# Five of eight repeats of a transformer block's attention stage, rolled from unrolled code into a hardware loop on four engines

## The reference, cut to what matters

```python
x = x + attention(layernorm(x), wq, wk, wv, wo)     # x: 8 sequences x 256 positions x 256
x = x + moe(layernorm(x), gate_w, w1, w3, w2, sw1, sw3, sw2)

# attention: 16 heads of 128, rotary embedding on q and k, causal softmax
q, k, v = (einsum('bsd,dnh->bsnh', x, w) for w in (wq, wk, wv))
q, k = llama_rope(q) / sqrt(128), llama_rope(k)
probs = softmax(where(causal, einsum('bqnh,bknh->bnqk', q, k), -1e30))
out = einsum('bqnh,nhd->bqd', einsum('bnqk,bknh->bqnh', probs, v), wo)

# moe: 8 experts of width 176, the best two of each token, and a shared expert of width 352
scores = softmax(x @ gate_w.T); topk_w, topk_idx = top_k(scores, 2)
y = sum over the two of w2_e(silu(w1_e x) * (w3_e x)) * topk_w / sum(topk_w)
y = y + (silu(x @ sw1) * (x @ sw3)) @ sw2
```

## Time and profile before

| what | value |
| --- | --- |
| median of three runs | 812.82 us |
| lowest and highest | 811.15 and 814.33 us |
| the profiled execution's own time | 814.33 us |
| its span, from first to last instruction | 812.5 us |
| mean granted TensorE clock | 0.980 |
| instructions in the trace | 16293 |

### The profile page before, as it was taken

One profiled execution on the slowest core, in us unless ns is written; L12 is line 12 of the kernel. 1 busy time (PEld: TensorE's weight loads), 2 busy tenths in 40 slices (PEclk: granted clock), 3 DMA queues, 4 the chain that ended last, 5 costly groups with the idle time before them and its releaser, 6 DMA issues.

```text
span 812.5 us, 16293 instructions
## 1 busy us (share of the span) xinstructions
PE 752.0 (93%) x5520; PEld 701.4 (86%) x5520; DVE 639.6 (79%) x1765; ACT 532.9 (66%) x1663; POOL 482.6 (59%) x508
## 2 busy tenths in 40 slices
PE   3799999999999999999999999999996879999994
PEld 3788999998998999899999989998885868888884
DVE  5698989988897998899888979988995574444447
ACT  4688777767776776777677767677886434555531
POOL 3578666676667666666766676667776261433300
PEclk9899999999999999999999999999999988999997
DMA  7254344444000000000000000001322213333373
GB/s 225 54 170 130 136 184 170 168 163 176 15 1 27 1 14 15 14 14 2 21 8 14 1 28 2 14 14 32 86 73 82 64 40 97 106 106 113 103 246 104
DMA packets 35753, 61.59 MB, mean 76 GB/s; under 512 B 6744, under 2 KB 27192, under 8 KB 35096
## 3 DMA queue, kind: packets, MB, share of 16 engines
q1 hardware_dynamic: 31624, 49.14, 18.6%
q0 software_dynamic: 4048, 11.42, 3.9%
HBM read 47.03 MB, written 32.46 MB: 98 GB/s over the span
## 4 chain that ended last, share of the span: by engine, by line
PE 57%; DVE 19%; POOL 11%; issue 5%; ACT 4%; DMA 3%; SPq 1%; POOLq 0%; DVEq 0%
PE bank L528 44%; DVE work L875 5%; POOL work L425 5%; PE bank L568 3%; POOL qkt_lo L1403 3%; PE bank L561 3%; DVE work L868 2%; PE bank L577 2%; DVE work L884 2%; PE bank L728 2%; POOL rows_by_expert L1516 2%; DVE pt_lo L896 2%; DMA stage<-in_L_attn_wk 1%; ACT qkt_hi L1223 1%; DVE w_lo L842 1%
## 5 line engine op out<-in xcount | busy, mean ns | idle before, releaser
L1403 POOL TENSOR_TENSOR qkt_lo<-work,qkt_hi 128x512 fp32r<-128x512 f32 x128 | 165.7, 1295 | 99.3 <-ACT qkt_hi L1223 99.3
L425 POOL TENSOR_TENSOR work<-work 128x512 f32<-128x512 f32 x127 | 165.3, 1302 | 72.0 <-DVE work L875 64.3
L875 DVE TENSOR_TENSOR work<-bank,sinn 64x512 f32<-64x512 f32 x256 | 176.2, 688 | 3.4
L528 PE MATMUL bank<-xnt_hi,w_lo 128*128 128x256 f32 x512 | 146.9, 287 | 3.2 <-POOL w_lo L1463 3.0
L1223 ACT CAST qkt_hi<-work 128x512 fp32r<-128x512 f32 x128 | 79.5, 621 | 103.1 <-POOL work L425 102.4
L528 PE MATMUL bank<-xnt_hi,w_hi 128*128 128x256 f32 x512 | 146.5, 286 | 0.0
L528 PE MATMUL bank<-xnt_lo,w_hi 128*128 128x256 f32 x512 | 146.5, 286 | 0.0
L1230 ACT ACTIVATE work<-work,bias 128x128 f32<-128x128 f32 (+1 forms) x256 | 112.6, 441 | 0.0
L868 DVE TENSOR_TENSOR work<-bank,cosn 128x512 f32<-128x512 f32 x128 | 87.8, 686 | 22.1 <-PE bank L528 22.0
L528 PEld LDWEIGHTS bank<-xnt_hi,w_lo 128*128 128x128 f32 x512 | 99.6, 195 | 3.9 <-DVE xnt_lo L906 3.3
L528 PEld LDWEIGHTS bank<-xnt_hi,w_hi 128*128 128x128 f32 x512 | 99.9, 195 | 0.0
(11 more groups left out here) (151 smaller groups left out, 2175.5 us busy)
## 6 DMA issues: line engine op xcount, KB each, us to landing
rows_by_expert<-in_zero_t SPq DMA_DIRECT2D x8, 2056.0 KB
stage<-rows_by_expert SPq DMA_DIRECT2D x39, 128.5 KB
stage<-in_L_ffn_w SPq DMA_DIRECT2D x32, 88.0 KB, 2.0
rows_by_expert<-in_zero_t SPq DMA_DIRECT2D x2, 1028.0 KB
resid<-in_L_attn_x SPq DMA_DIRECT2D x8, 256.0 KB, 3.8
stage<-in_L_attn_wq SPq DMA_DIRECT2D x8, 256.0 KB, 3.4
stage<-in_L_attn_wk SPq DMA_DIRECT2D x8, 256.0 KB, 4.2
stage<-in_L_attn_wv SPq DMA_DIRECT2D x8, 256.0 KB, 3.8
```

What stands on the lines that cost most here:

```text
L425: eng.tensor_tensor(roped[:, a], rope_cos[:, a], rope_sin[:, a], ALU.add).then_inc(rope_add, 1)
L528: mm = pe.matmul(out, lhs[a], rhs[b], start=start and n == 0, stop=stop and n == 2, skip_group_check=more)
L875: op = nc.vector.tensor_tensor(rope_sin[lo:lo + 64, a], p_qk[a][hi:hi + 64, :, :], sn, ALU.mult)
L1403: nc.gpsimd.tensor_tensor(qkt[a][1][:, :, :], roped[:, a], qkt[a][0][:, :, :], ALU.subtract).then_inc(qkt_lo, 1)
```

## The change

On PE, DVE, ACT and POOL the Python loop over b = 1 to 7 becomes: one unrolled call for b = 1, a hardware loop (`Fori`) for b = 2 to 6 whose body is in the stream once, and one unrolled call for b = 7. In the body, b is a value in a register of each engine. On DVE four waits get a `nop(nofuse=True)` behind them: one in each step of `sequence`, and one in each of the helpers `norm_mv`, `rows_stats` and `rows_mv`. They are in all eight sequences, in the loop and outside it.

```diff
@@ PE @@
             sequence(FIRST)
             pe.wait_ge(route_in, 64)
             pe.wait_ge(order_set, 1)
-            for b in range(1, B):
+
+            sequence(1)
+            with pe.Fori(2, LAST) as b:
                 sequence(b)
+            sequence(LAST)
@@ DVE @@
             def norm_mv(b):
                 dve.wait_ge(stats_done, b + 1)
+                dve.nop(nofuse=True)
                 for t in range(ST):
                     op = nc.vector.bn_aggr(mv[:, t, :], stats[:, t, :])
@@
                     if b is not LAST or h + 2 < N:
                         dve.wait_ge(s_ps, j0 + h + 3)
+                        dve.nop(nofuse=True)
                         mask_and_max((h + 2) % N)
@@
             def rows_stats(n, b):
                 dve.wait_ge(resid_done, n)
+                dve.nop(nofuse=True)
@@
             def rows_mv(n):
                 dve.wait_ge(stats2_done, n)
+                dve.nop(nofuse=True)
@@
             sequence(FIRST)
             dve.wait_ge(route_in, 64)
-            for b in range(1, B):
+
+            sequence(1)
+            with dve.Fori(2, LAST) as b:
                 sequence(b)
+            sequence(LAST)
@@ ACT @@
             sequence(FIRST)
-            for b in range(1, B):
+
+            sequence(1)
+            with act.Fori(2, LAST) as b:
                 sequence(b)
+            sequence(LAST)
@@ POOL @@
             pool.wait_ge(own_in, 16)
-            for b in range(1, B):
+
+            sequence(1)
+            with pool.Fori(2, LAST) as b:
                 sequence(b)
+            sequence(LAST)
             pool.wait_ge(scattered, 64 * (B - 1))
```

## The result

The changed kernel took 817.30 us (median of 4 runs, 816.66 to 818.66), the kernel before 812.52 beside it (4 runs, 811.15 to 814.33). The ratio is 1.0059, with an interval of 1.0035 to 1.0084: 4.8 us slower, between 2.8 and 6.8. The forecast was slower, 823.9: the direction is right, and the cost is less than half of the 11.1 us forecast.

The account below looks back on a forecast made before the run. The prediction took PE to bound the five looped sequences, with 1.1 us idle in each. Jumps 9.2 + 0.2, registers 1.7 and nops 0 made 11.1 us more, 823.9 us; own range 818 to 831, 8 in 10 815 to 837.

Parts of the forecast that it names:

- What it adds, 1: the jump back: At four loop borders each engine rereads its block; POOL's 2.3 us per jump reaches PE: 9.2 us, plus 0.2.
- only POOL stays resident: Rival on the loop's jumps, chance 0.12: only POOL still holds its block; the other engines miss theirs.
- the block is back before it is missed: Rival at the borders, chance 0.17: reads take little more than their packet, POOL alone pays 0.33 us per jump; 815.1 us.
- What is removed: Four copies of five sequences leave the stored instruction stream; fewer instruction packets to read gain 0.
- POOL: in full to PE: At the border POOL has no slack before its rotary sum, so its 2.3 us per jump reach PE in full.
- PE, DVE and ACT hidden at the border: Delays of 0.6 us on PE, 1.1 on DVE and 0 on ACT stay behind POOL's 2.3 and don't add.
- Register values: Making wait numbers in registers costs 0.087 us at four places per sequence, on POOL and DVE: 1.7 us; PE's hidden.
- The nops: On DVE, before the mask and in three helpers, the sequencer does them beneath running work: 0, at most 3.2 us.
- The sum: Whole kernel: 9.2 for jumps, 0.2 for branches, 1.7 for registers and 0 for nops, together 11.1 us.
- What would show it: POOL idle 2 us or more at four borders, sequences of 76.5 to 77 us, packets near 22 and 18.
- sign of being wrong: POOL's idle at the border stays near 0.1 us, or a pause on PE before line 568 is longer than POOL's.

Follow-up runs that it names:

- e6: Changed kernel with two sequences in each loop body on all four engines, so two jumps instead of four: 823.80 us against 812.60 before, ratio 1.0139.
- e1: The changed kernel measured a second time, with nothing altered: 817.56 us against 812.94 for the kernel before, ratio 1.0050.
- e5: Changed kernel with POOL's loop pass running from step 4 of a sequence to step 3 of the next: 816.69 us against 812.60 before, ratio 1.0057.
- e3: Changed kernel with POOL back to its unrolled stream; PE, DVE and ACT loop, nops kept: 815.24 us against 812.94 before, ratio 1.0035.
- e10: Kernel before with only PE looping, two sequences per body, no nops: 815.83 us against 812.37 before, ratio 1.0041.
- e11: Kernel before with only DVE looping, two sequences per body, with its nops: 816.84 us, ratio 1.0065 to before.
- e4: Kernel before, all engines unrolled, with only DVE's nops added: 812.75 us against 812.94 before, ratio 0.9994.
- e8: Changed kernel with POOL's transfers of steps 13 to 15 issued between rotary sum and low part: 810.10 us against 812.60 before, ratio 0.9973.
- e9: e6 with a hint on all four engines naming the jump back at the head of each pass: 818.65 us against 812.37 before, ratio 1.0109.
- e2: Kernel before with only POOL in the hardware loop, no nops: 815.92 us against 812.94 before, ratio 1.0033.
- e7: Kernel before, unrolled, with POOL's transfers of steps 13 to 15 issued between rotary sum and low part: 809.04 us against 812.60, ratio 0.9953.
- e12: e7 with the numbers of step 14's transfer also written ahead of step 14's sum: 807.42 us against 812.37 before, ratio 0.9944.

## Why the prediction was right in direction and wrong in size

The step that failed is **"What it adds, 1: the jump back"**, in its premise: "When a sequencer jumps to a block that it no longer holds, it must read it before going on." That much e6 shows: 3.46 us on DVE, with two 8 KB packets read in it. The premise that failed was that none is held: no run shows a miss with these bodies. All four are held: no packet is read in the four later passes. So the 2.3 us per jump, taken from the landing of a small transfer, had no transfer behind it. In its place the runs show 0.34 us for a jump with its count (e1 less e5; 0.25 against the loop's entry): 4 x 0.34 = 1.4 us instead of 9.2 + 0.2. This term alone is 8.0 us too high, more than the whole error of 6.3.

The nearest rival in its premise, "only POOL stays resident", had 0.12. It was right of POOL, but it let the others miss, and they didn't: DVE was not late (e3's border is as before). What I did not ask is how many blocks an engine holds beside the one it runs in; the trace before has no jump back and can't tell. The other rival of a cheap jump ("the block is back before it is missed", 815.1 and 0.17) was nearest in price, at 0.33 us per jump, with the wrong mechanism. The range for 8 in 10 began at 815, so it did hold 817.30; the forecast's own range, 818 to 831, did not.

In bytes, estimated by the forecast's 256 instructions per 16 KB on PE and 128 per 8 KB on the others: PE jumps back over 1170 instructions, 75 KB, without a packet and in 0.21 us, and misses at 150 KB (e6, e10). ACT missed some 400 instructions, 25 KB (e6), fewer bytes than PE held.

Point by point:

- **What is removed: 0.** Right. 30 packets less brought nothing: PE, DVE and ACT looping (e3) is no faster in any step.
- **POOL: in full to PE.** Right in place and in exchange: POOL's idle time grows by 0.52, and step 0 by 0.51 (4.76 to 5.27 in e1). The way was in part another one: ACT's rounding and PE's transposes of step 1 take the delay before the scores do.
- **PE, DVE and ACT hidden at the border.** Right as it came, in e3, but not tested at the price I gave. e11 shows what my price would have done: with a real miss, 2.8 us long, DVE's lateness is no 1.1 us behind POOL but 2.0 us on the path. The 3.1 us that I gave PE for a miss was 3.6 to 4.1, and in the sequences that one is indeed nearly hidden (0.3 us or less).
- **Register values: 1.7.** Found: 0.07 per sequence from POOL in step 14 (4.47 to 4.53 in e1, by the rounded medians), 0.09 from PE in step 10, 0.18 at each of four borders and 0.25 at the loop's entry: 5 x 0.16 + 4 x 0.18 + 0.25 = 1.8. The size was right; the places were POOL's, as listed, and one of PE's, which I had held to be hidden, and none of DVE's.
- **The nops: 0.** Wrong by little: 0.09 us per sequence, most of it in step 3 (4.54 to 4.60 in e4, where nothing else is changed), 0.4 us for the five. The whole time of e4 can't be told from before.
- **The sum.** 1.4 for the jumps, 1.8 for registers and 5 x 0.07 = 0.35 for the nops make 3.55; e1's five sequences grew by 3.47. The measured difference is 4.8 (2.8 to 6.8), and 1.3 of it, within the interval, has no place in the trace. The stages outside the five sequences vary from one execution to the next by 2 us and more. Yet what a kernel's whole time has beyond its sequences goes with PE's loop. It is 1.2 to 4.9 us in all seven in which PE loops: 1.2 in e1 and e8, 1.5 in e3, 2.3 in e5, and 2.8, 4.9 and 3.8 in e10, e6 and e9, whose body on PE is two sequences. It is -0.6, 0.3 and 0.3 in e4, e2 and e11, where PE is unrolled; the 1.1 and 1.2 of e7 and e12 are covered by their longer b = 1. The mean granted clock of e6 and e9 is also lower, 0.976 against 0.979 before, which may be a part of it. So PE's loop seems to cost something outside the five sequences too; where, and by what, stays open.
- **What would show it.** The list in the prediction wanted an idle of 2 us or more on POOL and sequences of 76.5 to 77 us; they were 0.60 and 74.95. Its sign of being wrong, an idle that stays near 0.1 us, didn't come either: 0.60 lies between the two. The packets, which were to stay near 22 and 18, were none, and their row alone decides the case.

## What to carry to other kernels

Before pricing a hardware loop, count the instructions of one pass on each engine, the sequencer's own included: up to the sizes shown here (1170 on PE, 256 on DVE, 201 on ACT, 210 on POOL) PE's branch took 0.21 us, POOL's jump with its count 0.34, and DVE's and ACT's jumps added no idle time at the border (DVE's next low part starts 0.06 us after the last one's end, 340.40 to 340.46 in the changed kernel); at the sizes tried past them (2340 on PE, some 500 on DVE, some 400 on ACT) a jump took 2.5 to 4.1 us. Between these sizes nothing was tried. Then look for the engines that have less slack where their jump stands than the jump takes. Here POOL had none, with 0.07 us between its last act and its next sum, and paid even for a held jump. DVE paid only for a missed one, and PE, whose sequencer was 1.8 us ahead, for little of that. And where a place without slack is found, the same reading is worth more turned round: moving three transfers out of it took 3.6 us off the unrolled kernel, and the loops then added only 0.9 us in the five sequences.

## What the runs showed of the hardware

- A held body is run again without any instruction traffic: 0 packets in 300 us, with a compare and branch of 213 ns on PE (median), 53 on POOL, and 0.22 us after it on POOL before the next operation. DVE's branch took 56 ns and ACT's 45 (medians). POOL's five, from the changed kernel:

```profile
L1558 POOLq FUSED_REGOPS  x5: 50/50/58, 189.5 to 490.6; - x5
L1558 POOLq COMPARE_BRANCH  x5: 44/53/57, 265.5 to 565.3; - x5
```

- A missed jump took 3.6 to 4.1 us on PE, 2.8 to 3.5 on DVE and 2.5 to 2.8 on ACT, more than any small transfer's landing in the earlier trace rows but the one at the cold start. With the hint ahead of the jump, PE's took 1.1 to 1.2.
- What a miss cost went with the engine here, not with its length: in the five sequences, 3.6 us or more of PE's sequencer cost 0.3 us or less, and 2.8 to 2.9 of DVE's cost 2.0.
- One indirect transfer of a sort that elsewhere lands in 2.6 us (median) took 8.63 us once, and PE stood idle behind it; the granted clock was 0.50 in the first 4.5 us of the sequence after it and 0.97 over the whole of it, which took 75.92 us against 74.70 in the profile of `e1_again`.
